# A four-layer graph network on one core: the transposing DMAs are issued by SyncE instead of ScalarE

## The chip, the cores and the metric

The kernel runs on one core of a Trainium2 chip. The core has five engines with a queue of instructions each: TensorE (matrix products, PE in the rows), VectorE (DVE), ScalarE (ACT), GpSimd (POOL) and SyncE (SP), which computes nothing and issues DMAs. They run side by side and wait for one another on semaphores. The metric is the device time of one execution in microseconds.

## What is computed

Four layers, each behind a layer norm and a relu, each added to x. x is 4096 x 256, adj is 4096 x 4096, float32.

```python
h = jnp.maximum(_layernorm(x, axis=-1), 0.0)
x = x + _L0_gnn_ref(h, adj, L0_gnn_W)            # relu(D (A+I) D ((A+I) h W^T))
h = jnp.maximum(_layernorm(x, axis=-1), 0.0)
x = x + _L1_gnn_ref(h, adj, L1_gnn_weight, L1_gnn_bias)
...
# L1: h = x @ weight; h_norm = h / norm(h)
#     attn = softmax(h_norm @ h_norm.T + log(adj + EPS)); out = attn @ h + bias
# L2: relu((D^-1/2 adj D^-1/2 @ x) @ W + b)
# L3: twice relu(concat([x, adj @ x]) @ W)
```

## The kernel before

**Passes.** adj is gone through six times. Pass 0 and 1 are the two products of L0, pass 2 (ATT) is the attention of L1, pass 3 is L2, passes 4 (TURNED) and 5 are L3. A pass has 8 groups (NG) of 512 output rows. In every pass but ATT a group has 8 chunks c of 1 MB of adj (512 x 512 float32). Each chunk is split into two float16 parts that together hold the float32 value: ScalarE makes the high part ahi (split, L771), VectorE the low part alo (L1035), and TensorE multiplies both (L489 and L490, or L492 to L494). In ATT a group has 32 blocks j: TensorE computes cosines into psS or transposes exponentials that an earlier group has sent to HBM (L669), ScalarE takes the exponential (L957), VectorE multiplies by adj (nums, L1250), ScalarE and VectorE split that (L974, L1257), TensorE multiplies.

**The tail.** When a group's products are done, its four accumulator banks are evacuated: in passes 1, 3 and 5 by ScalarE (o, L808) and VectorE, which adds the other half (L1043) and so frees the bank for the next group. The rest of the tail runs in places between the next group's chunks, listed in PLACES (by chunk) and ATT_PLACES (by block j), one table per engine. After the chunk's split of place 4 the "h" stage makes the normed rows hsp (ScalarE L856, VectorE L1149, which raises h_ready). Place "T", after the split of chunk 5, is turn_h: a DMA that transposes hsp (128 x 1024 float16) into hT. TensorE multiplies hT by the layer's weights ("W0W1", between chunk 5's second and third block of products, L582 or L590 to L592), waiting for hT_landed. Tails of pass 1 also need the rows divided by their norm for the attention's cosines: place 7, "n0" and "n1" (ScalarE L917, VectorE L1187, which raises gn_ready), and then "G", turn_gn, which transposes these rows into gnT, kept in the tile shared.

**Who issues what.** Loads of adj are issued by SyncE (load, L330; in ATT att_half, L380, for half chunks, with L388 for exponentials read back from HBM and send, L366, for exponentials sent there). A load of chunk c waits until the chunk four before it has been split, since the ring has four buffers. The transposing DMAs are issued by ScalarE: 24 of turn_h (L877; passes 1, 2 and 3) and 8 of turn_gn (L883; pass 1), from its own queue, in order with its computing.

Of the kernel before, what the change touches and what calls it, by code (L numbers as in the profile page):

```python
# [44 lines left out]
GB = 4  # L45
# [3 lines left out]
FB = F // P  # L49
# [23 lines left out]
def build(nc, x, adj_t, w0, wg, bias_g, w2, bias_2, w3a, w3b, sent, out):  # L73
# [4 lines left out]
    with ctx:  # L78
# [6 lines left out]
        def sem(name):  # L85
            return ctx.enter_context(nc.semaphore(name))
# [111 lines left out]
        x_ready = sem("x_ready")  # L198
        stats_ready = sem("stats_ready")
        passed = sem("passed")  # L200
        mv_ready = sem("mv_ready")
        var_ready = sem("var_ready")
        rstd_ready = sem("rstd_ready")
# [30 lines left out]
        def at(passes, p, g, per=1, k=1):  # L234
            return (g + NG * passes.index(p)) * per + k
# [78 lines left out]
        def _(sp):  # L314
# [4 lines left out]
            def load(p, g, c, first=False):  # L319
                if not first:  # L320

                    q, h, e = (p, g, c - 4) if c >= 4 else ((p, g - 1, c + 4) if not isinstance(g, int) or g > 0
                                                            else (p - 1, NG - 1, c + 4))
                    if q == ATT:

                        sp.wait_ge(num_ready, h * NB + (GB * (c + 7) if c < 2 else GB * (c + 5)))
                    else:
                        sp.wait_ge(split_ready, chunk_no(q, h, e) + 1)
                row = g * (NC * P) + c * P
                sp.dma_start(ring[c % 4], adj_t[bass.ds(row, P), :]).then_inc(adj_loaded[c % 4], 16)  # L330
# [17 lines left out]
                sp.dma_start(bg[:, :], bias_g[0:1, :].to_broadcast([P, F])).then_inc(b_loaded, 16)  # L348
                sp.dma_start(b2[:, :], bias_2[0:1, :].to_broadcast([P, F])).then_inc(b_loaded, 16)

            def group(p, g, first=False):
                for c in range(2 if first else 0, NC):
                    load(p, g, c, first=first and c < 4)
                    if first and c == 3:
                        load_others()
                    if p == 5 and c == 5 and not isinstance(g, int):
                        store(g - 1)
# [12 lines left out]
            def att_half(g, H):  # L370

                c = H // 2
                if g == 0 and H < 4:
                    sp.wait_ge(split_ready, chunk_no(ATT - 1, NG - 1, NC - 4 + c) + 1)
                else:

                    sp.wait_ge(num_ready, g * NB + HALF * (H - 3))
                row = (g * NC + c) * P
                cols = slice(H % 2 * HALF * GR, (H % 2 + 1) * HALF * GR)
                sp.dma_start(adj[:, c % 2, H % 2 * HALF:(H % 2 + 1) * HALF, :].rearrange("p b n -> p (b n)"),  # L380
                             adj_t[row:row + P, cols]).then_inc(half_loaded[H % 4], 16)
                if not computed(g, HALF * H):
                    exp_slot_free(sp, g, H)

                    for a in range(2):
                        sp.wait_ge(exp_sent[(2 * g + a) % 4], 32 * sent_no(c, 2 * g + a))
                    rows = sent_rows(c, g) + H % 2 * P
                    sp.dma_start(expo[:, H % 4, :], sent[rows:rows + P, :]).then_inc(exp_back[H % 4], 16)  # L388
# [10 lines left out]
            for p in range(6):  # L399
                if p == ATT:  # L400
                    for g in range(NG):
                        for H in range(NH):
                            before = (g, H - 4) if H >= 4 else (g - 1, H - 4 + NH)
                            if before[0] >= 0 and is_sent(*before):
                                send(*before)
                            att_half(g, H)
                else:
                    group(p, 0, first=p == 0)
                    with sp.Fori(1, NG) as g:
                        group(p, g)  # L410
# [337 lines left out]
        def _(act):  # L748
# [117 lines left out]
                                     (psT2 if r == 1 else psT)[:, :, :, :].rearrange("p b q n -> p (b q) n"), ACT.Copy)\  # L866
                    .then_inc(hT_kept, 1)

            def turn_h(p, g):

                act.wait_ge(h_ready, at(SMALL, p, g))

                if not isinstance(g, int) or g > 0:
                    act.wait_ge(small_ready, at(SMALL, p, g - 1, 2, 2))
                else:
                    act.wait_ge(small_ready, at(SMALL, SMALL[SMALL.index(p) - 1], NG - 1, 2, 2))
                act.dma_start_transpose(hT[:, :, :], hsp[:, :, :, :].rearrange("p b s n -> p (b s n)"))\  # L877
                    .then_inc(hT_landed, 16)

            def turn_gn(g):  # L880

                act.wait_ge(gn_ready, at([1], 1, g, GB, GB))
                act.dma_start_transpose(gnT[:, bass.ds(g * GB * 2 * FB, GB * 2 * FB), :],  # L883
                                        hsp[:, :, :, :].rearrange("p b s n -> p (b s n)")).then_inc(gnT_landed, 16)

            def small_out(p, b):

                return small_bank(p, b)[:, -F:]
# [31 lines left out]
            def stage(name, p, g):  # L920

                if name == "ev":
                    evacuate(p, g)
                elif name == "h":
                    if p == 0:
                        hi_of_t(p, g)
                    elif p in SMALL:
                        hi_of_h(p, g)
                elif name == "T":
                    if p in TURN:  # L930
                        turn_h(p, g)
                elif p in SMALL and name in ("W0", "W1"):
                    hi_of_small(p, g, int(name[1]))
                elif p == 1 and name in ("n0", "n1"):
                    hi_of_gn(p, g, int(name[1]))
                elif p == 1 and name == "G":
                    turn_gn(g)


            PLACES = {0: ["ev"], 4: ["h"], 5: ["T"], 6: ["W0", "W1"], 7: ["n0", "n1", "G"]}  # L940
            ATT_PLACES = [{2: ["ev"], 10: ["h"], 11: ["T"], 15: ["W0"], 16: ["W1"], 18: ["n0"], 19: ["n1"], 21: ["G"]},
                          {2: ["ev"], 17: ["h"], 18: ["T"], 26: ["W0"], 27: ["W1"]}]

            def group(p, g, tp, tg):
                for c in range(NC):
                    split(p, g, c)
                    for name in PLACES.get(c, []):
                        stage(name, tp, tg)
# [54 lines left out]
            for p in range(6):  # L1003
                if p == ATT:

                    act.wait_ge(dinv_ready, 2 * NG)
                    for g in range(NG):
                        att_group(g, *((ATT, g - 1) if g else (1, NG - 1)))
                    hi_of_numerators(NG - 1, NB - 1)
                else:  # L1010
                    if p > 0:
                        group(p, 0, p - 1, NG - 1)
                    if p in TURN:

                        for g in range(1, NG):
                            group(p, g, p, g - 1)
                    else:
                        with act.Fori(1, NG) as g:
                            group(p, g, p, g - 1)
            stage("ev", 5, NG - 1)  # L1020


# [337 lines left out]
```

## Time and profile before

| | |
|---|---|
| Median of 3 runs | 2461.54 us (2460.28 to 2462.68) |
| The profiled execution | 2456.39 us |
| Span of its instructions | 2454.6 us |
| TensorE busy | 2408.8 us, 98% |
| VectorE, ScalarE, GpSimd busy | 1450.2, 1082.2, 143.7 us |
| DMA | 490 MB, mean 200 GB/s |
| Mean granted clock of TensorE | 0.996 of full speed |

Times in the views are microseconds from the start of the span. A row of the timeline reads: start, duration, engine, line of the kernel, operation, written tile <- read tiles, shape, count, and in brackets how long the engine had been idle and what ended that. ACTq and SPq are DMA issues on the queues of ScalarE and SyncE: the duration is that of issuing; how long until the data has landed is told apart. Issues don't count as busy.

In this trace pass 1 runs from about 393 to 769, ATT to 1353, pass 3 to 1740, pass 4 to 2112.

### The profile page before, as it was taken

To read this page: it belongs to the slowest core of one execution; us is meant where nothing else is said; L and a number is where in the kernel's file an instruction comes from. 1 tells how busy PE (TensorE), PEld (TensorE's weight loads), DVE (VectorE), ACT (ScalarE), POOL (GpSimd) and SP (SyncE) were. 2 spreads that over 40 slices of the span, in tenths; PEclk is the share of its full clock that TensorE was granted. 3 is DMA by queue.
4 is the path that set the end of the run, shared out by engine and by line. 5 is a ranking of instruction groups with operands and counts; after the bars stand their busy time and mean duration, and the time that the engine had idled before them with its cause. 6 is when DMAs were issued, how large, how long until landed. Compare 5 with 4: busy or idle time off the path is not lost.

```text
span 2454.6 us, 41678 instructions
## 1 busy us (share of the span) xinstructions
PE 2408.8 (98%) x16584; PEld 1614.4 (66%) x16584; DVE 1450.2 (59%) x1907; ACT 1082.2 (44%) x1379; POOL 143.7 (6%) x114
## 2 busy tenths in 40 slices
PE   7999999999999999999999999999999999999999
PEld 7888887555556667777888666666544444566665
DVE  7645445675666566666777666566544454455555
ACT  6544444444444444444443444444444334443333
POOL 2300000111111000000000000001000000000000
PEclk9999999999999999999999999999999999999999
DMA  6455555656564866776778656555555445556553
GB/s 241 156 204 192 201 197 198 205 190 201 191 205 137 229 191 200 232 235 211 241 250 249 231 180 199 173 194 198 185 185 184 179 172 187 188 193 216 209 220 137
DMA packets 180289, 490.00 MB, mean 200 GB/s; under 512 B 80993, under 2 KB 114017, under 8 KB 139233
## 3 DMA queue, kind: packets, MB, share of 16 engines
q1 hardware_dynamic: 113344, 471.13, 55.5%
q10 hardware_dynamic: 66848, 17.57, 3.7%
q8 instruction: 63, 1.03, 0.2%
q14 instruction: 34, 0.27, 0.0%
HBM read 438.32 MB, written 33.55 MB: 192 GB/s over the span
## 4 chain that ended last, share of the span: by engine, by line
PE 90%; issue 3%; DVE 2%; ACT 2%; ACTq 1%; POOL 1%; DMA 1%; DVEq 0%; POOLq 0%
PE acc L489 25%; PE acc L490 12%; PE acc L493 8%; PE acc L492 8%; PE acc L494 8%; PE acc L502 5%; PE acc L500 5%; PE acc L501 5%; PE psS L683 2%; PE psS L685 2%; PE psS L684 2%; PE psS L669 2%; ACT ahi L771 1%; POOL rstd L432 1%; DMA hT<-hsp 1%
## 5 line engine op out<-in xcount | busy, mean ns | idle before, releaser
L489 PE MATMUL acc<-mov,ahi 128*128 128x512 f16 x3072 | 1004.2, 380 | 18.2 <-DVE o L1043 17.4
L490 PE MATMUL acc<-mov,alo 128*128 128x256 f16 x3072 | 839.5, 273 | 0.0
L1035 DVE SCALAR_TENSOR_TENSOR alo<-expo,ahi 128x2048 f16<-128x2048 f32 x160 | 366.6, 2291 | 348.4 <-ACT ahi L771 348.4
L492 PE MATMUL acc<-mov,ahi 128*128 128x258 f16 x2048 | 558.4, 273 | 4.8 <-DVE alo L1257 2.9
L493 PE MATMUL acc<-mov,ahi 128*128 128x256 f16 x2048 | 561.1, 274 | 0.0
L494 PE MATMUL acc<-mov,alo 128*128 128x258 f16 x2048 | 556.4, 272 | 0.0
L1035 DVE SCALAR_TENSOR_TENSOR alo<-adj,ahi 128x2048 f16<-128x2048 f32 x160 | 366.6, 2291 | 320.9 <-ACT ahi L771 318.8
L489 PEld LDWEIGHTS acc<-mov,ahi 128*128 128x128 f16 x3072 | 301.3, 98 | 383.6 <-DVE o L1043 19.8
L771 ACT ACTIVATE ahi<-expo 128x2048 f16<-128x2048 f32 x160 | 305.6, 1910 | 479.9 <-PE acc L490 297.5
L771 ACT ACTIVATE ahi<-adj 128x2048 f16<-128x2048 f32 x160 | 305.4, 1909 | 366.4 <-PE acc L490 178.4
L490 PEld LDWEIGHTS acc<-mov,alo 128*128 128x128 f16 x3072 | 301.3, 98 | 35.2
L492 PEld LDWEIGHTS acc<-mov,ahi 128*128 128x128 f16 x2048 | 196.9, 96 | 46.0 <-DVE alo L1257 5.6
L493 PEld LDWEIGHTS acc<-mov,ahi 128*128 128x128 f16 x2048 | 198.0, 97 | 39.5
L494 PEld LDWEIGHTS acc<-mov,alo 128*128 128x128 f16 x2048 | 202.1, 99 | 26.7
L974 ACT ACTIVATE ahi<-nums 128x512 f16<-128x512 f32 x256 | 160.0, 626 | 107.0 <-DVE nums L1250 102.0
L500 PE MATMUL acc<-ahi,mov 128*128 128x512 f16 x512 | 194.0, 379 | 0.0
L501 PE MATMUL acc<-alo,mov 128*128 128x512 f16 x512 | 194.0, 379 | 0.0
L502 PE MATMUL acc<-ahi,mov 128*128 128x512 f16 x512 | 194.0, 379 | 0.0
L1257 DVE SCALAR_TENSOR_TENSOR alo<-nums,ahi 128x512 f16<-128x512 f32 x256 | 175.2, 684 | 5.8 <-ACT ahi L974 5.7
L1250 DVE SCALAR_TENSOR_TENSOR nums<-adj,expo 128x512 f32<-128x512 f32 (+2 forms) x144 | 93.0, 646 | 131.3 <-ACT expo L957 130.8
L957 ACT ACTIVATE expo<-psS 128x512 f32<-128x512 f32 (+2 forms) x144 | 80.9, 562 | 201.9 <-PE psS L685 164.8
L432 POOL TENSOR_TENSOR rstd<-vare,neghalf 128x4 f32<-128x4 f32 x32 | 77.2, 2413 | 1160.2 <-DVE vare L1125 1160.2
(132 smaller groups left out, 2017.4 us busy)
## 6 DMA issues: line engine op xcount, KB each, us to landing
adj<-in_adj_t SPq DMA_DIRECT2D x160, 1024.0 KB, 4.8
expo<-in_adj_t SPq DMA_DIRECT2D x160, 1024.0 KB, 4.8
adj<-in_adj_t SPq DMA_DIRECT2D x128, 512.0 KB, 4.9
sent<-expo SPq DMA_DIRECT2D x112, 256.0 KB, 3.0
expo<-sent SPq DMA_DIRECT2D x56, 512.0 KB, 5.6
xres<-in_x SPq DMA_DIRECT2D x7, 512.0 KB, 10.0
out<-xres SPq DMA_DIRECT2D x7, 512.0 KB, 3.5
xres<-in_x ACTq DMA_DIRECT2D x1, 512.0 KB, 3.5
```

Of the source, the lines that this page charges most:

```text
L489: nc.tensor.matmul(acc[:, b, :].rearrange("p (s n) -> p s n", s=2), hi, both, start=first, stop=False)
L490: return nc.tensor.matmul(acc[:, b, 0:F], lo, m[:, jb, 0:F], start=False, stop=last)
L492: nc.tensor.matmul(acc[:, b, 0:n], hi, m[:, jb, 0:n], start=first, stop=False)
L493: nc.tensor.matmul(acc[:, b, 0:F], hi, m[:, jb, LO:LO + F], start=False, stop=False)
L494: return nc.tensor.matmul(acc[:, b, 0:n], lo, m[:, jb, 0:n], start=False, stop=last)
L500: nc.tensor.matmul(acc[:, f, :], hi, ahi[:, c % 2, k, :], start=first, stop=False)
L501: nc.tensor.matmul(acc[:, f, :], hi, alo[:, c % 2, k, :], start=False, stop=False)
L502: return nc.tensor.matmul(acc[:, f, :], lo, ahi[:, c % 2, k, :], start=False, stop=last)
L771: nc.scalar.activation(ahi[:, c % 2, :, :].rearrange("p b n -> p (b n)"), ring[c % 4], ACT.Copy, scale=ADJ_SCALE)\
L974: nc.scalar.activation(ahi[:, (j // GB) % 2, j % GB, :], nums[:, n % NUMS, :], ACT.Copy, scale=P_SCALE)\
L1035: nc.vector.scalar_tensor_tensor(alo[:, c % 2, :, :].rearrange("p b n -> p (b n)"), ring[c % 4], ADJ_SCALE, ahi[:, c % 2, :, :].rearrange( ...
L1257: nc.vector.scalar_tensor_tensor(alo[:, (j // GB) % 2, j % GB, :], nums[:, n % NUMS, :], P_SCALE, ahi[:, (j // GB) % 2, j % GB, :], ALU.mu ...
```

## The change

turn_h and turn_gn move from ScalarE's program to SyncE's, with the same waits (for h_ready or gn_ready, and for small_ready, that hT's last contents have been used). The stages "T" and "G" leave ScalarE's tables. SyncE issues turn_h behind the load of a group's chunk 0 and turn_gn behind that of its chunk 3; since loads run four chunks ahead, these stand at the splits of chunks 4 and 7 of the group before. So in the loop of pass 1 or 3 the load of group g carries the transposes of group g - 2, and the last two groups of a pass are turned in the next pass. In ATT the places are written out by hand (H counts half chunks, j = 2H). A semaphore, turning, is raised before each. ScalarE's groups of passes 1 to 3 ran from a written-out sequence where they issued the DMA and now run as a loop over registers.

```diff
+            def turn_h(p, g):
+
+                sp.wait_ge(h_ready, at(SMALL, p, g))
+                sp.wait_ge(small_ready, at(SMALL, p, g - 1, 2, 2))
+                sp.sem_inc(turning, 1)
+                sp.dma_start_transpose(hT[:, :, :], hsp[:, :, :, :].rearrange("p b s n -> p (b s n)"))\
+                    .then_inc(hT_landed, 16)
+
+            def turn_gn(g):
+
+                sp.wait_ge(gn_ready, at([1], 1, g, GB, GB))
+                sp.sem_inc(turning, 1)
+                sp.dma_start_transpose(gnT[:, bass.ds(g * GB * 2 * FB, GB * 2 * FB), :],
+                                       hsp[:, :, :, :].rearrange("p b s n -> p (b s n)")).then_inc(gnT_landed, 16)
+
-            def group(p, g, first=False):
+            def group(p, g, first=False, turned_rows=None):
                 for c in range(2 if first else 0, NC):
                     load(p, g, c, first=first and c < 4)
+                    if turned_rows is not None and c == 0:
+                        turn_h(*turned_rows)
+                    if turned_rows is not None and turned_rows[0] == 1 and c == 3:
+                        turn_gn(turned_rows[1])
...
                             att_half(g, H)
+
+                            if g == 0 and H == 1:
+                                turn_h(1, NG - 2)
+                            elif g == 0 and H == 3:
+                                turn_gn(NG - 2)
+                            elif g == 0 and H == 8:
+                                turn_h(1, NG - 1)
+                            elif g == 0 and H == 12:
+                                turn_gn(NG - 1)
+                            elif g > 0 and H == 11:
+                                turn_h(ATT, g - 1)
+                elif p in (1, 3):
+                    group(p, 0)
+                    group(p, 1, turned_rows=(ATT, NG - 1) if p == 3 else None)
+                    with sp.Fori(2, NG) as g:
+                        group(p, g, turned_rows=(p, g - 2))
+                elif p == TURNED:
+                    group(p, 0, turned_rows=(3, NG - 2))
+                    group(p, 1, turned_rows=(3, NG - 1))
+                    with sp.Fori(2, NG) as g:
+                        group(p, g)
...
-            PLACES = {0: ["ev"], 4: ["h"], 5: ["T"], 6: ["W0", "W1"], 7: ["n0", "n1", "G"]}
...
+            PLACES = {0: ["ev"], 4: ["h"], 6: ["W0", "W1"], 7: ["n0", "n1"]}
...
-                    if p in TURN:
-
-                        for g in range(1, NG):
-                            group(p, g, p, g - 1)
-                    else:
-                        with act.Fori(1, NG) as g:
-                            group(p, g, p, g - 1)
+                    with act.Fori(1, NG) as g:
+                        group(p, g, p, g - 1)
```

ScalarE, pass 1, from the split of a group's chunk 7 to the evacuation in the next group. Before:

```order
L771 ACTIVATE ahi<-expo 128x2048
L917 ACTIVATE hsp<-psW,rnorm 128x256 x2
L917 ACTIVATE hsp<-psT,rnorm 128x256 x2
L883 DMA_TRANSPOSE shared<-hsp 128x16x128
L771 ACTIVATE ahi<-adj 128x2048
L808 ACTIVATE o<-acc 128x256 x4
```

ScalarE at the same place, after. The rows up to the branch end the loop's body:

```order
L812 ACTIVATE ahi<-expo 128x2048
L935 ISA
L937 ISA
L939 REGISTER_ALU
L941 ACTIVATE hsp<-psW,rnorm 128x256 x2
L935 REGISTER_ALU
L937 REGISTER_ALU
L941 ACTIVATE hsp<-psT,rnorm 128x256 x2
L1032 REGISTER_ALU
L1032 COMPARE_AND_BRANCH
```

The DMA between the normalised rows and the next group's first split is gone; the loop goes on with that split.

SyncE, loop of pass 1, loads of chunks 3 and 4 of a group. Before:

```order
L328 REGISTER_ALU
L330 ISA
L330 DMA expo<-in_adj_t 128x2048
L328 ISA
L330 ISA
L330 DMA adj<-in_adj_t 128x2048
```

After:

```order
L329 REGISTER_ALU
L331 ISA
L331 DMA expo<-in_adj_t 128x2048
L362 ISA
L364 ISA
L364 DMA_TRANSPOSE shared<-hsp 128x16x128
L329 ISA
L331 ISA
L331 DMA adj<-in_adj_t 128x2048
```

The transpose of the normalised rows stands between the two loads, with its wait and the raising of turning (the two ISA rows).

SyncE, last group of ATT, around H = 11: half chunks of adj, exponentials read back, and after them the transpose. After the change:

```order
L408 DMA expo<-sent 128x1024
L357 DMA_TRANSPOSE hT<-hsp 128x16x128
L400 DMA adj<-in_adj_t 128x1024
L408 DMA expo<-sent 128x1024
L400 DMA adj<-in_adj_t 128x1024
```

Before, the load and the read-back of H = 12 (the third and fourth row) followed the read-back of H = 11 directly.

## Rows read from the trace of the kernel before

**Rows 1.** The page: busy time by engine, and the chain that ended last.

```profile
PE 2408.8 (98%) x16584; PEld 1614.4 (66%) x16584; DVE 1450.2 (59%) x1907; ACT 1082.2 (44%) x1379; POOL 143.7 (6%) x114
...
PE 90%; issue 3%; DVE 2%; ACT 2%; ACTq 1%; POOL 1%; DMA 1%; DVEq 0%; POOLq 0%
```

**Rows 2.** Waits of TensorE: for whom, us in total, times, longest.

```profile
PE acc L489 <- DVE o L1043: 17.4, 6, 4.3
...
PE acc L492 <- DVE alo L1257: 2.9, 2, 2.2
PE psW L582 <- DMA hT<-hsp: 2.3, 1, 2.3
PE psW L590 <- DMA hT<-hsp: 1.9, 1, 1.9
```

**Rows 3.** Timeline, pass 1, end of a group and start of the next.

```profile
566.94 0.84 ACT L917 ACTIVATE hsp<-psT,rnorm 128x256 f16<-128x256 f32 x2
...
569.35 0.87 DVE L1187 SCALAR_TENSOR_TENSOR hsp<-psT,rnorm,hsp 128x256 f16<-128x256 f32 x2
...
570.25 4.01 ACTq L883 DMA_TRANSPOSE shared<-hsp  x1
...
574.36 1.91 ACT L771 ACTIVATE ahi<-adj 128x2048 f16<-128x2048 f32 x1 [6.58 <-issue]
...
574.45 0.27 PE L490 MATMUL acc<-mov,alo 128*128 128x256 f16 x1
...
578.99 0.61 PE L489 MATMUL acc<-mov,ahi 128*128 128x512 f16 x1 [4.27 <-DVE o L1043]
```

**Rows 4.** Timeline, one group later.

```profile
621.89 1.91 ACT L771 ACTIVATE ahi<-adj 128x2048 f16<-128x2048 f32 x1 [3.90 <-issue]
...
626.52 0.39 PE L489 MATMUL acc<-mov,ahi 128*128 128x512 f16 x1 [1.59 <-DVE o L1043]
```

**Rows 5.** Windows: us, busy PE, PEld, DVE, ACT, POOL; clock, DMA share, GB/s.

```profile
578.70:582.20 3.50, 3.21 (x11) 1.54 (x12) 3.50 (x6) 0.46 (x1) 0.00 (x0) 0.51 0.65 227
1332.80:1336.30 3.50, 3.37 (x17) 2.66 (x18) 2.48 (x5) 1.26 (x2) 0.00 (x0) 0.54 0.64 117
1500.00:1600.00 100.00, 100.00 (x649) 63.34 (x648) 60.58 (x77) 45.55 (x50) 6.35 (x4) 1.00 0.56 190
```

**Rows 6.** Issue time ns min/median/max of the transposes; L877's and loads' landing.

```profile
L877 ACTq DMA_TRANSPOSE hT<-hsp x24: 1333/4214/4687, 455.3 to 1760.6; - x24
...
DMA to landing us min/median/max: 4.3/6.3/12.1
...
L883 ACTq DMA_TRANSPOSE shared<-hsp x8: 1332/1672/4007, 474.0 to 826.0; - x8
...
adj<-in_adj_t SPq DMA_DIRECT2D x160, 1024.0 KB, 4.8
```

**Rows 7.** Timeline, pass 3, start of its last group.

```profile
1687.66 1.91 ACT L771 ACTIVATE ahi<-adj 128x2048 f16<-128x2048 f32 x1 [3.29 <-PE acc L490]
...
1691.81 1.08 DVE L1043 SCALAR_TENSOR_TENSOR o<-acc,o 128x256 f32<-128x256 f32 x3
```

**Rows 8.** L877's DMA issued at 1428.72: time to landing.

```profile
DMA to landing us min/median/max: 9.6/9.6/9.6
```

**Rows 9.** Timeline, pass 1: load, transpose of h, first use of hT.

```profile
550.64 0.33 SPq L330 DMA_DIRECT2D adj<-in_adj_t  x1
551.60 4.26 ACTq L877 DMA_TRANSPOSE hT<-hsp  x1
...
558.94 0.27 PE L590 MATMUL psW<-wsp,hT 128*128 128x256 f16 x1
```

**Rows 10.** DMA queues between 551.6 and 554.5: packets, MB, share of 16 engines.

```profile
q1 hardware_dynamic: 106, 0.87, 90.6%
```

**Rows 11.** Timeline, last group of ATT: read-back of H = 12, transpose of h.

```profile
1325.01 0.37 SPq L388 DMA_DIRECT2D expo<-sent  x1
...
1327.33 3.81 ACTq L877 DMA_TRANSPOSE hT<-hsp  x1
```

More of the change, by code:

```diff
@@ L200, in build @@
         passed = sem("passed")
+        turning = sem("turning")
         mv_ready = sem("mv_ready")
@@ L867, in keep_hT @@
                     .then_inc(hT_kept, 1)
[L869 to L874, printed above, removed]
-                else:
[L876 to L884, printed above, removed]
             def small_out(p, b):
@@ L928, in stage @@
                         hi_of_h(p, g)
-                elif name == "T":
-                    if p in TURN:
-                        turn_h(p, g)
                 elif p in SMALL and name in ("W0", "W1"):
@@ L935, in stage @@
                     hi_of_gn(p, g, int(name[1]))
-                elif p == 1 and name == "G":
-                    turn_gn(g)
-            PLACES = {0: ["ev"], 4: ["h"], 5: ["T"], 6: ["W0", "W1"], 7: ["n0", "n1", "G"]}
-            ATT_PLACES = [{2: ["ev"], 10: ["h"], 11: ["T"], 15: ["W0"], 16: ["W1"], 18: ["n0"], 19: ["n1"], 21: ["G"]},
-                          {2: ["ev"], 17: ["h"], 18: ["T"], 26: ["W0"], 27: ["W1"]}]
+            PLACES = {0: ["ev"], 4: ["h"], 6: ["W0", "W1"], 7: ["n0", "n1"]}
+            ATT_PLACES = [{2: ["ev"], 10: ["h"], 15: ["W0"], 16: ["W1"], 18: ["n0"], 19: ["n1"]},
+                          {2: ["ev"], 17: ["h"], 26: ["W0"], 27: ["W1"]}]
             def group(p, g, tp, tg):
@@ L1012, in _ @@
                         group(p, 0, p - 1, NG - 1)
-                    if p in TURN:
-                        for g in range(1, NG):
-                            group(p, g, p, g - 1)
-                    else:
-                        with act.Fori(1, NG) as g:
-                            group(p, g, p, g - 1)
+                    with act.Fori(1, NG) as g:
+                        group(p, g, p, g - 1)
             stage("ev", 5, NG - 1)
```

## The prediction

> **What bounds the kernel now.** I read the page first: TensorE is busy for 98% of the span and 90% of the chain that ended last are its matmuls [rows 1]. So an edit on ScalarE and SyncE can only give back what TensorE does not use: its idle time, and time at its lower clock. The waits of TensorE come next [rows 2]. Leaving out the first 80 us and the last stores, which the change does not touch, four entries remain: 17.4 us in six waits for the addition that frees accumulator bank 0 (L1043, always at the start of a group of pass 1), 2.9 us in two waits in the attention pass, and two single waits of 1.9 and 2.3 us for the transposing DMA itself. (What is left, 1.4 us and less at changes of pass, I leave as it is.) Passes 0, 4 and 5 issue no transposing DMA and have none of these.
>
> The timeline then says what stands behind the six waits. VectorE finishes the last half of the normalised rows at 570.22 (569.35 + 0.87). ScalarE has had nothing to do since 567.78 (566.94 + 0.84), because turn_gn stands next on its queue and waits for those rows. At 570.25 it issues the DMA and needs 4.01 us for that; only at 574.36, after 6.58 us, comes the split of the next group's first chunk, and behind it the evacuation and VectorE's addition. TensorE ran out at 574.72 and starts again at 578.99, 4.27 us later [rows 3]. In every second group the issue takes 1.33 us and TensorE waits 1.59 us [rows 4]. Three long and three short waits make the 17.4.
>
> A long wait costs more than itself: just behind it the granted clock is 0.51 over 3.5 us, which is the 1.2 GHz level for nearly all of it; away from such waits it is the 2.4 GHz level [rows 5]. That is 3.5 x 0.49 = 1.7 us of lost work. I find five such stretches, each behind a wait of over 2 us: three in pass 1, one at 1332.8 in attention (0.54) [rows 5], one behind the 2.3 us wait. The waits of 1.6 and 1.9 us have none.
>
> **The change, part by part.**
>
> *ScalarE loses 32 issues and their waits.* 24 of them carry h (1.33 to 4.69 us each) and 8 the normalised rows (1.33 to 4.01) [rows 6]. Most lie beside TensorE's work and cost nothing. Those that count: with turn_gn gone the first split of a group waits only for its buffer, that is for TensorE's end of chunk 6. TensorE takes 5.2 us for a chunk (16 products, one every 0.325 us), so that is 574.7 - 5.2 = 569.5, and the split starts 4.8 us earlier than now; a stall of 4.27 fits into that with 0.5 us to spare. In the short case the split comes at 619.8 instead of 621.89, 2.1 us for a stall of 1.59, the same 0.5. What is late next? Pass 3 has the same start of a group, without turn_gn: split 1687.66, addition 1691.81 [rows 7], 4.15 us from split to addition, and TensorE waits nowhere between 1440 and 1770. By those distances pass 1 would have its addition at 573.7 and TensorE needs the bank at 574.7. VectorE is free at 570.22, before its split at 571.5. So I take all six: **17.4 us, and three stretches at the lower clock, 5.1 us.**
>
> *The two waits for hT.* The later one is for a DMA that is issued at 1428.72 and lands 9.6 us after that [rows 8], the other for one that takes 9.1; elsewhere in passes 1 and 3 it lands after 6.3 us and is used 7.3 us after its issue: 551.60, used at 558.94 [rows 9]. So of the 16 transposes of h between chunk passes 14 have only some 1.0 us to spare, and these two have none. From SyncE the DMA is issued at the same moment, since it waits for h_ready in both kernels, but on the queue that has just taken a load of 1 MB (550.64) [rows 9]. Is it then later? In the 2.9 us after the issue at 551.60 only the load's queue q1 moves packets, and none of q10 [rows 10]: already now it starts when the load is through, and one queue gives the same order. The late landings should even shorten, since the next load can no longer slip in ahead of its last packets. I take both waits and one slow stretch: **1.9 + 2.3 + 1.7 = 5.9 us**, bounds 0 and 5.9 (and below, in the rivals).
>
> A rule of the Trainium skill speaks against this: DMA: Bandwidth & Descriptors, "Queues, rings and completion order", says that a DMA engine takes turns between its rings packet by packet and goes through one ring in order. By it the transposes would now share the engines with the load and would afterwards have to queue behind it; what that would cost is the second rival. The row above shows no such turn-taking within those 2.9 us.
>
> *Attention.* ScalarE's issue of 3.81 us at 1327.33 [rows 11] is followed by its next conversion at 1331.5 and TensorE's wait of 2.2; the issue of 2.64 us one group earlier is followed by the wait of 0.7. Without them: **2.9 + 1.7 = 4.6 us**. But SyncE now stands at H = 11 until h is ready, and issues the DMA, before it sends and loads H = 12. In groups 1 to 6 this holds the pieces up by 2 to 6.5 us, and by their landings and first uses they have 9 to 14 us in hand. In group 7 it is tight: the read-back of H = 12 is issued at 1325.01 now [rows 11] and lands 6.3 us later; it would go out at 1328.7 + 0.4 to 1331.1 + 0.5 and land at 1335.4 to 1337.9, while TensorE wants it at 1339.46 - 2.2 - 1.7 = 1335.6. Between 0 and 2.3 us, and the transpose's packets lie ahead of it: I take **2.0 us lost**.
>
> *SyncE gains 32 issues.* Nothing else is queued behind them than loads. In passes 1 and 3 a load goes out at 550.64 and its split starts at 574.36 [rows 3, 9], with 4.8 us to land [rows 6]: 18 us in hand against an issue of at most 4.7. Nothing for that, nor for ScalarE's loops of registers, which passes 4 and 5 run without a wait.
>
> The Trainium skill, DMA: Bandwidth & Descriptors, "Issuing engines are not separate DMA queues", says that another issuing engine saves only the sequencer's time, usually small beside the DMA. By it, with an issue as short as a load's 0.33 us, the gain would be some 2 us. Here the sequencer's time is 1.33 to 4.69 us against a landing of 6.3 [rows 6], and it stands on the path six times.
>
> **The sum.** 17.4 + 5.1 + 5.9 + 4.6 - 2.0 = 31.0 us. The profiled execution has a span of 2454.6 and took 2456.39 us, 5 us less than the median of 2461.54; I take the difference off the median: **2430.5 us**, and off the span: 2423.6.
>
> **Rivals.**
>
> 1. *The starts of pass 1's groups come back, the hT waits or group 7 don't.* 22.5 to 27 us gained: 2434.5 to 2439. For it: group 7 hangs on differences of a microsecond. I count it with the forecast, as the upper side of that case.
> 2. *One queue puts the transpose a microsecond later.* If it may start only when the load has landed (550.64 + 4.8 = 555.4) and then needs its shortest landing of 4.3 us [rows 6], it lands at 559.7 where TensorE asks at 558.94: 0.8 us of waiting, 16 times, 13 us, and the 5.9 are not won. 31.0 - 5.9 - 13 = 12 us gained: 2449.
> 3. *Slower: the transposes land late as a rule.* Landings of 9.1, 9.6 and 12.1 us exist. If all 16 in passes 1 and 3 landed after 9.6, TensorE would wait 9.6 - 7.3 = 2.3 us each time and lose 1.7 at the lower clock: 64 us against 25 gained, 2500. It decides from 25/16 = 1.6 us beyond the 7.3, a landing of 8.9 us. Against it: 14 of the 16 land within 6.8 us, with a load in flight before and one behind.
> 4. *The issue is not what holds ScalarE* and something else ends those 6.58 us. Then nothing moves: 2461. The idle time is marked "issue" in [rows 3] and shrinks to 3.90 with the issue in [rows 4], which speaks against it.
>
> **How the numbers follow.** What this kernel's measurement can tell from no change is about 0.2%, 5 us. Forecast with rival 1: 0.80. Rival 2: 0.10 (faster too). Rival 3: 0.07, less a little that ends near zero. Rival 4 and small mixtures: 0.03. Faster 0.89, same 0.04, slower 0.07. The range takes the forecast's case, 33 us gained and the upper side of rival 1, with 1 to 3 us for the spread of runs, and a part of rival 2: 2425 to 2443.
>
> **What would show it.** No wait of TensorE on L1043 in pass 1 over 1 us, and ScalarE's split of a group's first chunk released by TensorE's end of chunk 6; no stretch below clock 1.00 between 80 and 1440; SyncE with 32 DMA_TRANSPOSE of 1.3 to 4.7 us; landings of at most 7.3 us in passes 1 and 3. In group 7 of attention, one wait on the read-back of up to 2 us. The prediction is wrong if TensorE waits for hT in many groups, or if the starts of pass 1's groups keep a wait because VectorE's split or addition comes late for another reason.

## The result, and the profile after

The changed kernel takes 2425.36 us (median of 4 runs, 2424.70 to 2426.42) against 2460.91 us for the kernel before (4 runs, 2457.95 to 2462.68): a ratio of 0.9857, 95% interval 0.984 to 0.9874. That is 35.5 us less between the medians, and 30.0 us less between the two profiled spans (2454.6 and 2424.6).

First the page of the kernel after: span, busy time by engine, the queues, and the chain that ended last.

```profile
span 2424.6 us, 41920 instructions
...
PE 2402.9 (99%) x16584; PEld 1612.9 (67%) x16584; DVE 1451.9 (60%) x1907; ACT 1084.5 (45%) x1379; POOL 143.7 (6%) x114
...
q1 hardware_dynamic: 179904, 487.91, 59.3%
...
q10 hardware_dynamic: 288, 0.79, 0.1%
...
PE 96%; issue 2%; POOL 1%; DVE 0%; ACT 0%; DMA 0%; POOLq 0%; DVEq 0%; ACTq 0%
```

The transposes' packets have moved from q10 to q1, the queue of the loads. TensorE's matmuls are 96% of the chain instead of 90% [rows 1], and ScalarE's issues have left it.

TensorE's waits after (for whom, us in total, times, longest), the largest first:

```profile
PE acc L755 <- DVE vare L1139: 6.5, 1, 6.5
PE psT L590 <- DVE ev L1163: 3.3, 4, 1.4
PE psT L590 <- DVE hsp L1163: 3.2, 3, 2.1
PE acc L533 <- DVE o L1057: 1.5, 1, 1.5
PE acc L530 <- DVE alo L1049: 0.7, 1, 0.7
...
PE psS L710 <- DMA expo<-sent: 0.4, 1, 0.4
```

The four entries of [rows 2], 24.5 us together, are gone. The first three lines here belong to the first 80 us and stood there before (6.7, 3.0 and 3.2 us); the fourth, at attention's start, was 1.4 us. One line is new: 0.4 us for a read-back of exponentials.

The same place as in [rows 3], the end of a group of pass 1 and the start of the next, timeline of the kernel after:

```profile
562.89 0.87 DVE L1201 SCALAR_TENSOR_TENSOR hsp<-psT,rnorm,hsp 128x256 f16<-128x256 f32 x2
563.15 1.91 ACT L812 ACTIVATE ahi<-adj 128x2048 f16<-128x2048 f32 x1 [1.83 <-PE acc L531]
563.97 3.76 SPq L364 DMA_TRANSPOSE shared<-hsp  x1
...
567.30 1.08 DVE L1057 SCALAR_TENSOR_TENSOR o<-acc,o 128x256 f32<-128x256 f32 x3
568.03 0.34 SPq L331 DMA_DIRECT2D adj<-in_adj_t  x1
...
568.48 0.38 PE L530 MATMUL acc<-mov,ahi 128*128 128x512 f16 x1
```

ScalarE's split is now released by TensorE's chunk 6 (563.15), 5.33 us ahead of the next group's first matmul (568.48), which follows without a wait. VectorE's addition comes 4.15 us behind the split, as in pass 3 [rows 7], and ends its first bank some 0.8 us before TensorE needs it. The issue still takes 3.76 us, but on SyncE. The load behind it goes out at 568.03, 0.3 us after the issue's end; the split that it also waits for is through at 567.38 (timeline: VectorE's part, 565.09 + 2.29), so it is late by some tenths of a microsecond at most.

The issues of the transposes after, and the landings of those of h:

```profile
L357 SPq DMA_TRANSPOSE hT<-hsp x24: 1707/4066/5192, 456.9 to 1731.1; - x24
...
DMA to landing us min/median/max: 4.3/5.8/7.4
...
L364 SPq DMA_TRANSPOSE shared<-hsp x8: 1692/3736/3873, 475.5 to 802.2; - x8
```

The issue got no shorter (median 4.07 us, before 4.21 [rows 6]); it is now in a place where it costs nothing. The longest landing fell from 12.1 to 7.4 us.

The clock, in windows of the kernel after (us, busy times, then clock, DMA share and GB/s):

```profile
31.00:35.00 4.00, 4.00 (x31) 3.11 (x32) 2.69 (x13) 1.94 (x2) 1.12 (x2) 0.60 0.44 35
460.00:745.00 285.00, 285.00 (x1811) 176.98 (x1809) 194.95 (x271) 144.24 (x210) 42.15 (x33) 1.00 0.64 206
750.00:756.00 6.00, 4.67 (x22) 2.69 (x23) 3.44 (x9) 1.53 (x6) 0.00 (x0) 0.72 0.54 171
```

Pass 1 is at 1.00 and without a gap. Two slow stretches are left in this execution: one in the start-up, which the profile of before did not have there, and one behind the 1.5 us wait at attention's start. (Two more traces of the changed kernel have neither.) They cost 4.00 x 0.40 = 1.6 and 6.00 x 0.28 = 1.7 us. So between the two profiles 24.5 us of waits go and 0.4 come, and five stretches of 1.7 us become two: 24.1 + 8.5 - 3.3 = 29.3 us, against 30.0 measured.

### The profile page after: what moved, and what is told of

Its sections match the earlier page's. It is cut to its first block, busy times and chain, and to the rows that moved or that the text cites. A ratio compares the mean times of both kernels' runs of the same rounds, so it can differ in the third digit from the quotient of the medians.

```text
span 2424.6 us, 41920 instructions
## 1 busy us (share of the span) xinstructions
PE 2402.9 (99%) x16584; PEld 1612.9 (67%) x16584; DVE 1451.9 (60%) x1907; ACT 1084.5 (45%) x1379; POOL 143.7 (6%) x114
## 4 chain that ended last, share of the span: by engine, by line
PE 96%; issue 2%; POOL 1%; DVE 0%; ACT 0%; DMA 0%; POOLq 0%; DVEq 0%; ACTq 0%
PE acc L530 27%; PE acc L531 14%; PE acc L534 9%; PE acc L535 9%; PE acc L533 9%; PE acc L543 5%; PE acc L541 5%; PE acc L542 5%; PE psS L724 2%; PE psS L725 2%; PE psS L726 2%; PE psS L710 2%; POOL rstd L473 1%; PE psS L633 1%; PE psS L631 1%
```

## The experiments

**My theory** was that ScalarE's issue of the transposes, in order with its computing, is the cost: at the starts of pass 1's groups, twice in attention, and for hT through the second queue. **The rivals**: ScalarE's standing wait for VectorE is the cost and not the issue; it is ScalarE's loops, which the change rewrites too; it is only the place in the order, so that the engine doesn't matter; or the late landings of hT have another reason than the two queues. The kernels ran in three series, each on one chip and with the kernel before beside them; times are compared within a series. The kernel before had a median of 2457.64 us in the first (13 runs, 2452.80 to 2464.59; the next four experiments), 2458.76 in the second (7 runs, 2455.30 to 2462.37; the changed kernel again, the groups written out, H = 12, the held load) and 2459.13 in the third (7 runs, 2454.86 to 2467.51; the rest).

### Only the transposes of the normalised rows on SyncE

The kernel before, with SyncE's code from the change but without its turn_h, and ScalarE without turn_gn.

```diff
-                elif p == 1 and name == "G":
-                    turn_gn(g)
...
+                    if turned_rows is not None and turned_rows[0] == 1 and c == 3:
+                        turn_gn(turned_rows[1])
```

> The kernel before, but the 8 transposes of the normalised rows (turn_gn) are issued by SyncE as in the changed kernel; the 24 of h stay on ScalarE. If the issue of turn_gn on ScalarE is what stops TensorE at the starts of pass 1's groups, the six waits on L1043 (17.4 us) and the three stretches at the lower clock (5.1 us) go, and the waits in attention (2.9 us) and those for hT (up to 4.2 us, with late landings of 9 us or more) stay: a span of about 2432 us, some 22 us less than before. If it is the number of DMA queues that matters (two queues still carry transposes and loads), less than half of it comes back: above 2443.

Measured: 2433.74 us (2430.32 to 2441.48), ratio 0.9916 (0.989 to 0.9942), span 2430.0. No wait on the addition in pass 1 is left; the two waits in attention are there (3.3 us) and so are two for hT (1.3 and 2.5 us). The span is 24.6 us below that of the kernel before's profile, where 22.5 had been reckoned; of the 2.1 us between, 1.7 are a slow stretch that the waits for hT do not have behind them this time. **8 of the 32 transposes carry most of the gain.** One of hT's two late landings is the same as before, the seventh of pass 1: issued at 720.6, landed after 8.6 us (before at 743.6, 9.1 us). The other has moved, from the second of pass 3 (1428.72) to the seventh:

```profile
1640.04 4.77 ACTq L913 DMA_TRANSPOSE hT<-hsp  x1
...
1649.74 0.28 PE L618 MATMUL psW<-hT,wsp 128*128 128x256 f16 x1 [2.48 <-DMA hT<-hsp]
```

The seventh of pass 1 is late in all three traces in which ScalarE issues the transposes of h and the loads run free (8.6 to 9.1 us). So only a part of the late landings has a fixed place, and the four runs lie 11 us apart.

### Only the transposes of h on SyncE

```diff
-                elif name == "T":
-                    if p in TURN:
-                        turn_h(p, g)
...
+                    if turned_rows is not None and c == 0:
+                        turn_h(*turned_rows)
```

> The kernel before, but the 24 transposes of h (turn_h) are issued by SyncE; the 8 of the normalised rows stay on ScalarE. If the costs simply add up, the six waits at the starts of pass 1's groups stay (17.4 us and the slow stretches behind the long ones), and the waits in attention (2.9 us) and for hT (4.2 us) go, with up to two slow stretches and less 0.4 us for the new wait in attention's last group: about 10 us less than before, a span near 2445 us. The late landings of hT (9.1 and 9.6 us) are gone, all at most 7.4 us. If the late landings have nothing to do with the two queues, they stay and the gain is 4 us.

Measured: 2459.37 us (10 runs, 2458.09 to 2461.89), ratio 1.0006 (0.9996 to 1.0017): **nothing gained, where I expected 10 us.** The waits for hT and for VectorE in attention went as expected, with no landing over 6.7 us but in the transposes left on ScalarE. But the waits at pass 1's starts grew, and those for read-backs in attention are 2.5 us instead of the 0.4 allowed:

```profile
PE acc L526 <- DVE o L1066: 22.5, 6, 4.2
...
PE psS L706 <- DMA expo<-sent: 2.5, 3, 1.3
```

The timeline of ScalarE's queue says why (start, duration of the issue):

```profile
475.46 3.91 ACTq L909 DMA_TRANSPOSE shared<-hsp  x1
...
526.48 3.93 ACTq L909 DMA_TRANSPOSE shared<-hsp  x1
...
577.59 3.96 ACTq L909 DMA_TRANSPOSE shared<-hsp  x1
...
628.76 1.33 ACTq L909 DMA_TRANSPOSE shared<-hsp  x1
...
674.75 3.85 ACTq L909 DMA_TRANSPOSE shared<-hsp  x1
...
724.95 3.87 ACTq L909 DMA_TRANSPOSE shared<-hsp  x1
```

Every fourth transpose on this queue is issued in 1.33 us, the others take 3.9. Before, the transposes of h stood between them, so that every second one of these was a fourth; alone, it is one of six. Five stalls are long now, not three. And behind the first of them the lower clock lasts longer than in [rows 5]:

```profile
482.40:489.20 6.80, 5.10 (x17) 2.44 (x18) 6.65 (x10) 1.88 (x2) 0.00 (x0) 0.51 0.57 173
```

Here the clock falls while TensorE still waits: it works for 5.10 of these 6.80 us, so that 5.10 x 0.49 = 2.5 us of work are lost, against 3.21 x 0.49 = 1.6 in [rows 5]. Four of the five stretches of pass 1 are of this length. That is 5.1 us more in waits, some 7 us more at the lower clock there, 2.5 us of read-backs and a slow stretch in the start-up (1.7), some 16 us in all; the h side gives 7.1 us of waits and two slow stretches, 10.5. The span is 5.5 us longer than the kernel before's. The two halves of the change don't add up.

One more thing stands in these runs: the long waits are all there, but the ten times lie within 3.8 us, where those of the kernel before, on the same chip, lie over 11.8.

### The issue on SyncE, the waits still on ScalarE

```diff
+                elif name == "T" and p in TURN:
+                    act.wait_ge(h_ready, at(SMALL, p, g))
+                elif name == "G" and p == 1:
+                    act.wait_ge(gn_ready, at([1], 1, g, GB, GB))
...
+            PLACES = {0: ["ev"], 4: ["h"], 5: ["T"], 6: ["W0", "W1"], 7: ["n0", "n1", "G"]}
...
```

> The changed kernel, but ScalarE keeps the two waits at the old places (for h_ready after chunk 5's split, for gn_ready after the normalised rows); only the issue is SyncE's. Theory 1, the issue of 1.3 to 4 us is the price: ScalarE is released at the moment VectorE ends the rows, 0.7 us after chunk 6's end, with 0.5 us to spare, so TensorE waits at most 0.3 us per group: within 2 us of the changed kernel. Theory 2, the standing wait of 2.5 us for VectorE is the price: about half or more of the 17.4 us come back as waits, and the kernel lands 9 to 20 us above the changed one.

Measured: 2430.85 us (2429.57 to 2431.76), ratio 0.9896 (0.9878 to 0.9913), span 2428.6. In pass 1 ScalarE's split is held until VectorE is done, and TensorE waits a little (timeline):

```profile
566.01 1.91 ACT L812 ACTIVATE ahi<-adj 128x2048 f16<-128x2048 f32 x1 [2.96 <-DVE hsp L1205]
...
570.64 0.39 PE L530 MATMUL acc<-mov,ahi 128*128 128x512 f16 x1 [0.59 <-DVE o L1061]
```

Six waits of 0.6 us, 3.6 us in all, and no slow stretch behind them. The span is 4.0 us above the changed kernel's; between the medians it is 5.5 us (2425.36), but these two were measured apart. Two to three times what I allowed, and still under the 9 to 20 of the rival: the standing wait costs some 4 to 5.5 us, **the issue the rest of the 22.5.**

### turn_gn one chunk later, all on ScalarE

```diff
                 elif p == 1 and name == "G":
+                    if g > 0:
+                        turn_gn(g - 1)
+                elif p == 1 and name == "G8":
                     turn_gn(g)
...
-            PLACES = {0: ["ev"], 4: ["h"], 5: ["T"], 6: ["W0", "W1"], 7: ["n0", "n1", "G"]}
+            PLACES = {0: ["ev"], 1: ["G"], 4: ["h"], 5: ["T"], 6: ["W0", "W1"], 7: ["n0", "n1"]}
...
```

> The kernel before with all transposes on ScalarE; only turn_gn stands one chunk later, behind the split of the next group's chunk 1 (in attention behind block 3; the last one as before). If the cost is the place in ScalarE's order and not the issuing engine, the starts of groups in pass 1 come free as in the changed kernel. ScalarE is idle for 3.3 us before each split in mid-group, against an issue of 4 us at most, so a split may come 0.7 us late, of which 0.5 us are covered: 20 to 22 us less than before, a span of 2432 to 2435 us. If any issue of 4 us on ScalarE costs its time in pass 1, at most 5 us are gained.

Measured: 2434.68 us (2430.26 to 2435.12), ratio 0.9906 (0.9886 to 0.9925), span 2433.0, within what was expected. The issue lies in ScalarE's pause now:

```profile
568.77 4.33 ACTq L883 DMA_TRANSPOSE shared<-hsp  x1
568.96 1.90 ACT L771 ACTIVATE ahi<-adj 128x2048 f16<-128x2048 f32 x1
573.93 1.91 ACT L771 ACTIVATE ahi<-expo 128x2048 f16<-128x2048 f32 x1 [3.08 <-PE acc L490]
```

and no wait on the addition is left in pass 1. So 22 of the 35 us need no other engine, only **another place in ScalarE's order**. What SyncE adds are the waits in attention (5.0 us here, with one slow stretch behind the longer of them) and those for hT (3.2 us here, with none). That the split at 568.96 runs beside the issue is no contradiction to [rows 3]: it is the split of chunk 1, which stands ahead of turn_gn in ScalarE's program; the row of an issue can begin before the instruction ahead of it is through. The split that stands behind the issue here is that of 573.93, 0.8 us after the issue's end (568.77 + 4.33), and TensorE's products release it.

### The changed kernel again, and ScalarE's groups written out

> The changed kernel once more, beside the kernel before and the next three on the same chip. Theory: with one queue for loads and transposes the landings of hT no longer vary, so its runs lie within 3 us of one another (those before lay over 12 us in the last call), at 2425 to 2427 us. If the small spread was chance, it spreads like before, over 8 us or more.

Measured: 2424.96 us (2423.17 to 2427.71), ratio 0.9866. The spread is 4.5 us, more than the 3 I gave it, less than the 7.1 of the kernel before beside it.

The second kernel takes back the loops alone:

```diff
-                    with act.Fori(1, NG) as g:
-                        group(p, g, p, g - 1)
+                    if p in TURN:
+                        for g in range(1, NG):
+                            group(p, g, p, g - 1)
+                    else:
+                        with act.Fori(1, NG) as g:
+                            group(p, g, p, g - 1)
```

> The changed kernel with ScalarE's groups of passes 1 to 3 written out again, as they were before; the transposes stay on SyncE. This is the other half of the change taken back alone. If the loops cost or bring nothing, the time is that of the changed kernel within 1 us. If ScalarE's register work in the loops cost time at the starts of groups, it is 1 to 3 us faster.

Measured: 2424.49 us (2422.76 to 2426.88), against 2424.96: **the loops cost and bring nothing.** All of the gain is the transposes'.

### Attention's last transpose behind H = 12

```diff
-                            elif g > 0 and H == 11:
+                            elif g > 0 and H == (12 if g == NG - 1 else 11):
```

> The changed kernel, but in attention's last group SyncE issues the transpose of h behind the load and read-back of H = 12 instead of ahead of them. The wait of TensorE for that read-back (0.4 us in the changed kernel, predicted 2.0) goes, since the read-back goes out some 6 us earlier; nothing else moves: 0 to 1 us faster than the changed kernel.

Measured: 2422.86 us (2422.24 to 2425.86) against 2424.96. The wait in the last group is gone; one of 0.6 us in an earlier group stays. The difference of the medians, 2.1 us, is within the spread of either kernel, so the time does not settle it; only the wait does.

### The next load held until hT has landed

The kernel with only turn_gn on SyncE; turn_h stays on ScalarE's queue. Where the change would issue turn_h, SyncE waits for its landing:

```diff
+            def turn_h(p, g):
+                sp.wait_ge(hT_landed, 16 * at(TURN, p, g))
+                sp.sem_inc(turning, 1)
```

> The kernel with only turn_gn on SyncE (its runs lay between 2430 and 2441 us, with hT landing after 8.6 and 9.6 us in two places), and in addition SyncE holds the next load in passes 1, 3 and at their edges until hT has landed; ScalarE still issues the transposes of h, on its own queue. If the late landings come from the next load's packets, which get in ahead of the transpose's last ones on the other queue, then in passes 1, 3 and 4 all 16 land within 7 us, TensorE has no wait for hT, and the runs lie within 4 us of one another, near 2429 us. If they come from something else, landings over 8 us and the spread of 8 us or more stay.

Measured: 2429.20 us (2426.51 to 2431.22), ratio 0.9882. Landings of the transposes of h in pass 3, then in pass 1:

```profile
DMA to landing us min/median/max: 6.2/6.4/6.4
...
DMA to landing us min/median/max: 6.1/6.5/6.6
```

The longest at the edges of the passes is 7.0 us, TensorE waits for hT nowhere, and the runs lie 4.7 us apart instead of 11. In attention, where the load is not held, landings of 8.5 and 12.7 us stay.

The trace of the kernel before shows it at the transpose of [rows 8], issued at 1428.72. Packets by queue from 1431 to 1435, then from 1435 to 1438:

```profile
q10 hardware_dynamic: 2048, 0.52, 73.4%
q1 hardware_dynamic: 79, 0.52, 43.8%
...
q1 hardware_dynamic: 125, 0.91, 74.5%
q10 hardware_dynamic: 32, 0.00, 0.6%
```

By 1435, 6.3 us after its issue, all but 32 small packets of the transpose are through, and those take until the next load's packets are nearly all moved. **The late landings come from the next load on the other queue.**

### The transpose of h a load later, and ahead of its load

Both on the changed kernel, one run each.

```diff
-                    if turned_rows is not None and c == 0:
+                    if turned_rows is not None and c == 1:
```

> The changed kernel, but in the chunk passes SyncE issues the transpose of h behind the load of chunk 1 instead of chunk 0, some 4.9 us later. This doubles the disputed thing, how late hT may be. If hT has about 1.1 us to spare, TensorE waits 3.5 to 4 us for it in each of 15 groups, 55 us, with a slow stretch behind each (1.7 us, or 3.4 as behind the long waits of the kernel with only turn_h moved): a span of 2500 to 2530 us. If hT has more to spare than its landing tells, under 20 us are lost.

Measured: 2527.13 us, some 102 above the changed kernel. TensorE's waits:

```profile
PE psW L623 <- DMA hT<-hsp: 35.4, 8, 4.7
PE psW L631 <- DMA hT<-hsp: 31.7, 7, 4.7
```

67 us in 15 waits of 4.5, each followed by a slow stretch. The first of these DMAs is issued 4.8 us later (461.7, changed kernel 456.9), and as a rule they land after 7.1 us instead of 5.8. In the changed kernel hT lands 0.9 to 1.6 us ahead of its first use in the chunk passes, and 0.1 us ahead for the first one of pass 3 (issued at 1358.5): so little is there to spare.

```diff
+                    if turned_rows is not None and c == 0:
+                        turn_h(*turned_rows)
                     load(p, g, c, first=first and c < 4)
-                    if turned_rows is not None and c == 0:
-                        turn_h(*turned_rows)
```

> The changed kernel, but in the chunk passes SyncE issues the transpose of h ahead of the load of chunk 0 instead of behind it; it starts when h is ready, as before, and the load 2 to 4 us later. If the transpose's 6 us to landing are partly the load in front of it on the same queue, it now lands after 4.3 to 4.7 us and hT has 2.5 us or more to spare. If the 6 us are its own, nothing changes. The time stays within 2 us of the changed kernel either way, since loads have 18 us in hand.

Measured: 2424.70 us, the changed kernel's time. The landings in pass 1 (at 460 to 700), all but equal:

```profile
DMA to landing us min/median/max: 4.3/4.3/4.3
```

Of the 5.8 us after the change 1.5 are the load in front of the transpose. Without it hT has some 2.9 us to spare. The load goes out later by 3.4 us (2.27 us behind the transpose's start at 543.78, where it was 1.16 us ahead of one at 545.30), out of its 18. A load right behind the transpose on the same queue does not make it late.

### The evacuation one block earlier at attention's start

The kernel with attention's last transpose behind H = 12, and in both engines' first table of attention the stage "ev" at block 1 instead of 2.

```diff
-            ATT_PLACES = [{2: ["ev"], 10: ["h"], 15: ["W0"], 16: ["W1"], 18: ["n0"], 19: ["n1"]},
+            ATT_PLACES = [{1: ["ev"], 10: ["h"], 15: ["W0"], 16: ["W1"], 18: ["n0"], 19: ["n1"]},
...
```

> The kernel with attention's last transpose behind H = 12, and in addition the evacuation of pass 1's last group stands behind block 1 instead of block 2 at attention's start (ScalarE and VectorE). This is aimed at the last wait of size outside the first 80 us, 1.5 us at attention's start, which in some runs is followed by a slow stretch of 1.7 us. If the evacuation's place ends that wait, it shrinks to under 0.5 us: 1 to 3 us faster than the changed kernel. If the first numerators end it, it stays or grows.

> The changed kernel again, as the one to compare with on the same chip: 2424 to 2427 us.

Measured: 2422.65 us (2421.52 to 2423.97), ratio to the kernel before 0.9849 (0.9825 to 0.9874), and the changed kernel beside it 2424.11 us (2423.58 to 2427.32), ratio 0.9856. The 1.5 us wait is gone from the list, a wait of 0.6 on an exponential has come. This has the lowest median of all versions, 1.5 us below the changed kernel and 0.2 us below the one with H = 12 alone (2422.86, in the second series); both are within the spread of the runs. The profile, not the time, says that the earlier evacuation is better.

## Why the prediction was right, and where it was off

2430.5 us was forecast and 2425.36 measured, 0.4 us above the lower end of the range (2425 to 2443). That it lies inside is luck in part: in the second and third series the changed kernel's medians were 2424.96 and 2424.11, just below it. By its steps:

- **The starts of pass 1's groups: right.** All six waits (17.4 us) went, with the three slow stretches (5.1 us). The 0.5 us that it gave TensorE's bank as slack is 0.8 in the rows of after. Moving turn_gn alone gave 24.6 us of span, 22.5 of them here, and keeping ScalarE's wait but not the issue cost 4.0 to 5.5.
- **The two waits for hT: right, for a reason that was only half seen.** The transpose starts behind the load in either case, but [rows 10] could not show it alone: their window ends at 554.5, and q10's first packet moves at 554.9, with q1's last ones of that load until 555.6. The second experiment on the transpose's place says it: on one queue the load in front costs it 1.5 us. The Trainium skill, DMA: Bandwidth & Descriptors, "Queues, rings and completion order", says that a ring is gone through in order, and that engines take turns between rings; the first is what the 4.3 and 5.8 us show, and the second is what the 32 last packets between 1435 and 1438 and the held load show at the transpose's end. That rule, which I had set against the change, speaks for it.
- **Attention: right in kind, small in size.** 2.9 us of waits and one slow stretch went. The loss in the last group was put at 2.0 us and is 0.4; that the change would put the transpose ahead of the tightest read-back is seen, and moving it back ends the wait. The 2.0 took over ScalarE's issue of 3.81 us and a landing of 6.3; from SyncE the issue there takes 1.71 us and the read-back lands after 5.3. The 9 to 14 us in hand that it gave groups 1 to 6 were too many: in another profile of the changed kernel a read-back of an earlier group is waited for by 1.4 us.
- **Loads and loops: right**, nothing for either (the kernel with the groups written out).
- **The sum against the profile: 31.0 forecast for the span, 30.0 measured.** Two slow stretches that it did not count, in the start-up and at attention's start, stand against the smaller loss in the last group. The second of them is against the sign "no stretch below clock 1.00 between 80 and 1440".
- **The step that failed: "I take the difference off the median".** The median of before was 5 us above its profiled run, and I treated that as a constant that both kernels share. It is not: the changed kernel's median is 1.1 us below its own profiled run (2426.42). About half of the 5 us did not come again: in the three later series the median of before is only 1.3 to 2.7 us above the 2456.39 of that profiled run. The rest belongs to what the change removes, as far as the spreads tell: with h's transposes on ScalarE's queue and the load free, runs of one kernel lie 7.1, 11.2, 11.8 and 12.7 us apart in four sets, 4.7 and 4.9 in two others; with them on the load's queue, or with the load held, never more than 4.7, in the ten runs of the kernel with only turn_h moved 3.8. That the landings vary between executions of one kernel is inferred, since the kernel before was traced once; and the six waits for hT seen in three traces are of 1.3 to 2.5 us, with a slow stretch behind one of them, which does not by itself fill 12 us. The forecast should have asked why the runs differ before carrying the difference over.
- **A part that was never in the forecast**: I had counted halves of the change as if each had its own price. The kernel with only turn_h moved shows that they are coupled through the issue times on ScalarE's queue: alone, that half is worth nothing.

Rivals 2 and 3, in which the transpose lands later from SyncE's queue, are excluded by the landings (at most 6.4 us in pass 1, 7.4 at one edge). Their kind of price is real: with hT 4.8 us later the kernel takes 2527 us, 6.8 us more for each of 15 groups. Rival 4 is excluded by the kernel with the waits kept. Rival 1's losses did not come: hT is not waited for, and group 7 loses 0.4 us.

## What to carry to other kernels

A DMA issue is an instruction of the engine that issues it, and a transposing one took 1.3 to 5.3 us here: look for it on the queue of any engine whose next instruction the bottleneck waits for, and first try another place in that queue, then an engine that computes nothing. If a small DMA has little time to spare and a large one follows it, put both on one queue, the small one first. Where runs of a kernel differ by more than usual, find out what varies before a change is priced against their median.

## What the runs showed of the hardware

- On ScalarE's queue every fourth transposing DMA is issued in 1.33 us in the chunk passes, and the others take 3.9 to 4.8 us between loads; in attention and at pass 3's start the fourth took 1.33 to 2.4 us. It holds for the mixed sequence of before, for the 24 of h alone, and for the 8 of the normalised rows alone, where there are two such fourths (1.33 and 1.39 us). On SyncE's queue, among loads, there is no such fourth: 3.4 to 5.2 us in the chunk passes, and 1.7 to 2.2 us as a rule where nothing has just been issued ahead (in attention, and in the kernel with the transpose ahead of its load). The cause stays open.
- The short issue does not make the landing short: that of 1.33 us at 1573.3 in the kernel before landed after 6.4 us, like its neighbours.
- The same DMA (128 x 1024 float16, SBUF to SBUF) lands after 4.3 us alone, as a rule 5.2 to 6.8 behind a 1 MB load (7.0 to 7.4 at pass 3's start, and with the transpose a load later), and in the chunk passes 8.6 to 9.6 us, in attention up to 13.4, where the next load on another queue gets in before its end.
- Behind waits of about 4 us in pass 1 the granted clock was at its lower level for 3.4 us or for 6.8; in the kernel with only turn_h moved both lengths occur, and of the 6.8 some 1.7 lie within the wait. Behind the waits of 0.6 us there was no such stretch, and behind waits of 1.3 to 2.5 us there was one in some cases and none in others.
